# Self-attention of a four-layer Perceiver on one core: scores as row tiles of 32 with masked queries, the bias table added by TensorE, four batches in a group

## The reference, cut to what matters

```python
h = layernorm(x)
q, k, v = heads(h @ Wq), heads(h @ Wk), heads(h @ Wv)      # (16, 16, 64, 16)
s = einsum('bhqd,bhkd->bhqk', q, k) * scale + table[h]     # 64 x 64, -inf above the diagonal
x = x + merge(einsum('bhqk,bhkd->bhqd', softmax(s), v)) @ Wo
```

## Time and profile before

| | us |
|---|---|
| median of 3 runs | 4456.29 |
| lowest, highest | 4456.26, 4457.72 |
| the profiled execution's own time | 4445.81 |
| its span in the trace | 4444.5 |
| mean granted TensorE clock | 0.928 |

### The profile page before, as it was taken

How to read it: one execution, slowest core, us unless ns; L and a number is a source line. 1 busy time by engine, 2 the same in 40 slices (tenths; PEclk the granted TensorE clock), 3 DMA queues, 4 the chain that set the end, 5 groups by cost and what they waited for, 6 DMA issues and landing times. The chain is left out here.

```text
span 4444.5 us, 98901 instructions
## 1 busy us (share of the span) xinstructions
PE 3904.2 (88%) x40956; PEld 3176.0 (71%) x40956; DVE 2984.3 (67%) x7518; ACT 2129.4 (48%) x2970; POOL 1683.7 (38%) x1714
## 2 busy tenths in 40 slices
PE   8999999746999999777899999945797999999766
PEld 6888887425888888447788888823796888888446
DVE  6777777675777777562677777748445777777644
ACT  4555555243555555231455455522463555555334
POOL 3444432201332332320565656413684332322237
PEclk9999999877999999885899999976798999999868
DMA  3212212001111110000211111000552111110025
GB/s 89 61 53 61 53 49 92 16 22 48 31 43 35 39 39 24 22 20 1 78 61 54 46 61 53 24 16 2 186 195 75 37 40 35 43 31 24 16 85 178
DMA packets 126302, 237.48 MB, mean 53 GB/s; under 512 B 10000, under 2 KB 115104, under 8 KB 122016
## 3 DMA queue, kind: packets, MB, share of 16 engines
q1 hardware_dynamic: 118464, 174.11, 13.2%
q0 software_dynamic: 7392, 57.06, 3.7%
HBM read 210.15 MB, written 20.97 MB: 52 GB/s over the span
## 5 line engine op out<-in xcount | busy, mean ns | idle before, releaser
L598 ACT COPY prob_t<-ps 128x1024 f32<-128x1024 f32 x512 | 518.2, 1012 | 1180.1 <-PE ps L485 1180.1
L485 PE MATMUL ps<-c_ident,prob 128*128 128x128 f32 (+1 forms) x6656 | 920.3, 280 | 12.4 <-ACT prob L736 10.6
L485 PEld LDWEIGHTS ps<-c_ident,prob 128*128 128x128 f32 (+1 forms) x6656 | 712.1, 141 | 204.7 <-issue 183.0
L736 ACT ACTIVATE prob<-prob,nmx 128x1601 f32<-128x1601 f32 x512 | 828.6, 1625 | 1.1 <-DVE nmx L649 1.1
L501 PE MATMUL ps<-ctx,wk 128*128 128x400 f32 (+1 forms) x3072 | 688.6, 360 | 25.5 <-DVE vals L608 18.4
L515 PE MATMUL ps<-wv,ctx 128*128 128x256 f32 x4992 | 706.4, 290 | 3.1 <-DVE vals L608 3.1
L515 PEld LDWEIGHTS ps<-wv,ctx 128*128 128x128 f32 x4992 | 619.2, 186 | 16.4 <-DVE vals L608 4.0
L640 DVE CUSTOM_DVE_ANT_0 prob<-ps,mk 128x400 f32<-128x400 f32 (+2 forms) x1024 | 526.2, 570 | 104.0 <-PE ps L473 99.3
L598 DVE COPY prob_t<-ps 128x1024 f32<-128x1024 f32 (+1 forms) x384 | 402.4, 1048 | 270.2 <-PE ps L485 270.2
L643 DVE TENSOR_SCALAR_CACHE_REDUCE prob<-ps 128x400 f32<-128x400 f32 (+2 forms) x1024 | 526.2, 570 | 85.3 <-PE ps L473 79.9
L501 PEld LDWEIGHTS ps<-ctx,wk 128*128 128x128 f32 x3072 | 535.5, 191 | 44.2 <-DVE vals L608 32.9
(11 more groups left out here) (343 smaller groups left out, 4622.8 us busy)
## 6 DMA issues: line engine op xcount, KB each, us to landing
raw_ctx<-in_ctx_t SPq DMA_DIRECT2D x120, 400.0 KB, 3.3
raw_ctx<-in_ctx_t SPq DMA_DIRECT2D x60, 402.0 KB, 5.2
raw_ctx<-in_ctx_t SPq DMA_DIRECT2D x60, 399.0 KB, 3.2
mk<-in_mask_f SPq DMA_DIRECT2D x32, 400.2 KB, 5.4
mk<-in_mask_i SPq DMA_DIRECT2D x16, 800.5 KB, 4.4
sorted<-zeros SPq DMA_DIRECT2D x2, 3840.0 KB, 19.7
rows<-sorted SPq DMA_DIRECT2D x30, 256.0 KB, 5.3
done<-done SPq DMA_DIRECT2D x30, 256.0 KB, 2.5
```

The source lines that it names most:

```text
L485: mm = pe.transpose(ps[0:w, turn_bank(u, i) + a, r * P:(r + 1) * P], prob[u % 2][:, r, x * P:x * P + w], cst['ident'][:])
L598: copy(prob_t[0:w, ring(u, i), 0:nb, :], ps[0:w, turn_bank(u, i):turn_bank(u, i) + nb, :]).then_inc(st[sem], 1)
L736: a.activation(prob[h % 2][:, r, :], prob[h % 2][:, r, :], ACT.Exp, bias=nmx[:, r:r + 1], accum_out=den[h % 2][:, r:r + 1]).then_inc(st['e ...
```

## The change

The core takes groups `G` of four batches, so there are 4 groups in place of 8 pairs.

Scores: in place of masked keys, ACT makes masked queries once for the whole stage: `qm` holds for each pair of neighbouring heads the queries with the other head's 16 rows set to zero. A matmul then contracts 32 rows only, for 2 heads of one batch, and the four groups of 32 rows (`r`) go to four banks of PSUM. The table is added by PE: a matmul of an identity matrix with the table, in the type fp32r, starts each bank, and the scores accumulate on it. For layer 0 the table is in two parts, high and low, so two such matmuls a bank. DVE takes the largest straight from four banks of PSUM (2048 elements a row), subtracts it on the way to SBUF in two halves of 1024, and sums in the same halves. POOL still does the multiplication by the reciprocals.

Values: `vals` holds them in two copies, one for each head of a pair, with zeros in place of the other's; POOL clears it and ACT fills it from PSUM, with SiLU where the layer has it, so that `early_act` and its barrier are gone. Each multiplication by the values takes 16 small matmuls for a transposed part of 4 x 128 columns, where 16 served a whole `u` before.

Output: ACT copies the heads out; the projection of a group (`out`) is done by PE inside the loop, behind the scores of the next group, and DVE adds it to `X` (`add_out`) two groups late, within the loop. The projection uses the PSUM banks of the transposes, so that the first two transposes of group `G` wait for `x_added` of group `G - 1`.

```diff
-    vmask = st.tile("vmask", [P, D])
+    NB = ROWS if L == 0 else 1
+    bias = st.tile("table", [P, NB, 256])
+    bias_parts = [st.tile(f"table{i}", [P, NB, 256], F32R) for i in range(2 if L == 0 else 1)]
...
+    def begin_pool():
+        p = nc.gpsimd
+        p.memset(vals[:], 0.0).then_inc(st['zeroed'], 1)
+        p.tensor_copy(ident_r[:], cst['ident'][:])
+        p.wait_ge(*st.at('weights', 16 * n_loads))
+        p.tensor_copy(bias_parts[0][:], bias[:]).then_inc(st['table_hi'], 1)
...
+        def scores(G):
+            if G:
+                pe.wait_ge(*st.at('shifted', 2 * G))
+            else:
+                pe.wait_ge(*st.at('q_masked', 4 * C))
+            for r in range(ROWS):
+                for i, part in enumerate(bias_parts):
+                    row = part[:, r % part.shape[1], :].unsqueeze(1).broadcast_to([P, 2, 256])
+                    pe.matmul(ps[:, r, :].rearrange("p (a n) -> p a n", a=2), ident_r[:], row, start=(i == 0), stop=False)
+            for a in range(2):
+                for g in range(C):
+                    for bb in range(2):
+                        b, u = 4 * G + 2 * a + bb, UNITS * a + 2 * g + bb
+                        for r in range(ROWS):
+                            rows = slice(32 * r, 32 * r + 32)
+                            mm = pe.matmul(ps[:, r, u * S:(u + 1) * S], qm[rows, g, b].rearrange("p h s -> p (h s)"),
+                                           kt[rows, g, b * S:(b + 1) * S], start=False, stop=(u == 2 * UNITS - 1))
+            mm.then_inc(st['ss_mm'], 1)
...
+            if G and i < 2:
+                pe.wait_ge(*st.at('x_added', 2 * (G - 1) + i + 1))
...
+        scores(0)
+        values()
+        for G in range(GROUPS):
+            if G + 1 < GROUPS:
+                scores(G + 1)
+            if G:
+                out(G - 1)
+            for i in range(4):
+                turn(G, i)
+                if i:
+                    weighted(G, i - 1)
+            weighted(G, 3)
+        out(GROUPS - 1)
...
+        for G in range(GROUPS):
+            largest(G)
+            for a in range(2):
+                shifted(G, a)
+            for a in range(2):
+                totals(G, a)
+            if G >= 2:
+                for u in range(2):
+                    add_out(2 * (G - 2) + u)
+        for t in range(2 * (GROUPS - 2), T):
+            add_out(t)
...
+        exponentials(0)
+        for G in range(GROUPS):
+            if G + 1 < GROUPS:
+                exponentials(G + 1)
+            for i in range(4):
+                a.wait_ge(*st.at('st_mm', 4 * G + i + 1))
+                if 4 * G + i >= 2:
+                    a.wait_ge(*st.at('so_mm', 4 * G + i - 1))
+                a.copy(pt[i % 2][:], ps[:, TURN + i % 2, :]).then_inc(st['pt'], 1)
+            a.wait_ge(*st.at('so_mm', 4 * (G + 1)))
```

More of the change, by code:

```diff
@@ L917, in self_attention @@
     layernorm_act(k, st)
+    begin_pool()
+    st.made(zeroed=1, table_hi=1)
     if row:
@@ L942, in self_attention @@
     OT = st.tile("heads_out", [P, C, NT])
[L943 to L991, removed]
+    qm = st.tile("q_masked", [P, C, B, 2, S])
@@ new lines, in weighted @@
+        def weighted(G, i):
+            a, g = i // 2, i % 2
+            pe.wait_ge(*st.at('pt', 4 * G + i + 1))
+            if i == 0:
+                pe.wait_ge(*(st.at('ot', OUTS * G) if G else st.at('values', 2 * T // 2)))
+            for h in range(2):
+                for bb in range(2):
+                    rows = slice(bb * S, bb * S + S)
+                    for r in range(ROWS):
+                        j = 4 * g + r
+                        mm = pe.matmul(ps[32 * r:32 * r + 32, OUT + bb, i * S:(i + 1) * S],
+                                       vals[rows, 2 * G + a, h, 32 * j:32 * j + 32],
+                                       pt[i % 2][rows, r * P + h * S:r * P + h * S + S], start=(h == 0), stop=(h == 1))
+            mm.then_inc(st['so_mm'], 1)
@@ new lines, in act @@
+        for n in range(T // 2):
+            a.wait_ge(*st.at('sv_mm', n + 1))
+            if n == 0:
+                a.wait_ge(*st.at('zeroed', 1))
+            for h in range(2):
+                o = vals[:, 2 * n:2 * n + 2, h, :].rearrange("p t (j h d) -> p t j h d", h=2, d=HD)[:, :, :, h, :]
+                s = ps[:, TURN + n, :].rearrange("p (t j h d) -> p t j h d", t=2, h=2, d=HD)[:, :, :, h, :]
+                a.activation(o, s, ACT.Silu if L == 2 else ACT.Copy).then_inc(st['values'], 1)
@@ new lines, in exponentials @@
+        def exponentials(G):
+            for x in range(2):
+                p = pr[G % 2][:, :, units(x), :]
+                a.wait_ge(*st.at('shifted', 2 * G + x + 1))
+                a.activation(p, p, ACT.Exp).then_inc(st['sexp'], 1)
+        exponentials(0)
[4 more added lines that the diff above has]
+                a.wait_ge(*st.at('st_mm', 4 * G + i + 1))
+                if 4 * G + i >= 2:
+                    a.wait_ge(*st.at('so_mm', 4 * G + i - 1))
+                a.copy(pt[i % 2][:], ps[:, TURN + i % 2, :]).then_inc(st['pt'], 1)
+            a.wait_ge(*st.at('so_mm', 4 * (G + 1)))
+            for bb in range(2):
+                o = OT[:, :, 256 * G:256 * G + 256].rearrange("p g (x b q) -> p x g b q", x=2, b=2)[:, :, :, bb, :]
+                s = ps[:, OUT + bb, 0:256].rearrange("p (x g q) -> p x g q", x=2, g=C)
+                if bv is None:
+                    a.copy(o, s).then_inc(st['ot'], 1)
+                else:
+                    for g in range(C):
+                        a.activation(o[:, :, g, :], s[:, :, g, :], ACT.Identity, bias=bv[:, g:g + 1]).then_inc(st['ot'], 1)
@@ L1120, in self_attention @@
     pool()
[L1121 to L1129 removed]
+    st.made(q_masked=4 * C, sv_mm=T // 2, values=T, ss_mm=GROUPS, smax=GROUPS, shifted=2 * GROUPS, sexp=2 * GROUPS,
+            total=2 * GROUPS, rtotal=2 * GROUPS, probs=2 * GROUPS, st_mm=4 * GROUPS, pt=4 * GROUPS, so_mm=4 * GROUPS,
+            ot=OUTS * GROUPS, o_mm=T, x_added=T)
     nc.all_engine_barrier()
```

219 lines of the change are left out of this document (86 added, 133 removed).

## The result

The change makes the kernel faster, by 1.2 to 1.3%: median 4396.05 us (4391.08 to 4396.63, four runs) against 4456.27 us (4452.0 to 4457.72, four runs), a ratio of 0.9866 with a 95% interval of 0.985 to 0.9881, 60 us. A second comparison gave 4394.29 for 4447.19 us, 0.9878 (0.9861 to 0.9894), 53 us. The two traces, of executions of 4396.63 and 4445.81 us, lie 49.2 us apart.

What follows compares the result with a forecast made beforehand. DVE's list bounds the cores before, a ring of waiting engines after; cores 40 us less plus 3 around them make 43, median 4456.3 to 4413 us. Forecast 4400 to 4428 (chance 0.55), range 4383 to 4441.

Steps and rivals of the forecast that it cites:

- the high clock: Rival, chance 0.15: PE's clock stays high in the cores; ring 17.1 us, kernel 4382 or so.
- What bounds it: In layer 0's core DVE's list sets the pipeline's round; its work falls from 72 to 38 us a core.
- The ring: In the cores, DVE 8.5, PE 4.7, clock 2.5 and scores 3.9 us follow without overlap: 19.6 us in layer 0.
- the low clock: Rival, sharing chance 0.2 with costlier rings: clock stays low through all of PE's part; about 25 us, 4438.
- Layer 0's core: Start, one full ring and end of layer 0's self-attention core add up to 88.0 us, where before took 87.7.
- my 49.0: Layer 0's core: us into it when DVE's 8.5 us behind group 2's scores end, ahead of one ring of 19.6.
- What closes the ring: PE's transposes of groups 1 and 2 are released by DVE's addition to X, with some 7 us of idling each.
- Layer 2: Layer 2's core goes from 122.0 to 86 us, 36 less, as the separate phase for the values goes.
- The small score matmuls: A group's 32 score matmuls of 32 rows overlap in four row tiles and take 2.2 us, bounds 1.3 and 2.9.
- The rival's 92 us: Rival, chance 0.07: small score matmuls do not overlap, 8.8 us a group, 92 us in four cores, kernel 4505.
- Around the cores: Outside the cores: 3 us less for four stages, bounds 0 and 6; POOL's clearing costs nothing.
- The median: 43 us less takes the profiled 4445.81 to 4403 us and the median 4456.3 to 4413.

Runs made afterwards that it cites:

- the run of layer 2 alone: Layer 2's self-attention as in the kernel after, layers 0, 1 and 3 as before; 4413.92 us, ratio 0.9913 to before.
- copies first: After with DVE's additions to X one turn earlier and ACT's four copies of a group ahead of the next exponentials; 4340.45 us, ratio 0.9752 to before.
- combined: The copies first kernel plus POOL's clearing later and the first group's table matmuls ahead of the wait for masked queries; 4318.95 us, ratio 0.9707 to before.
- the extra matmuls in groups 1 and 2: After with ten unread matmuls behind the output projection, only in the turns of groups 1 and 2; 4387.64 us, ratio 0.9853 to before.

## Why the prediction was right, and where its sizes were off

Against its own trace the sum said 43 us less, and the traces say 49.2. Against the median it said 4413 us, and 4396 was measured: inside the range of 4383 to 4441, but 4 us below the forecast of 4400 to 4428 that had the chance of 0.55. The range was also written a little carelessly: it is said to take in the high clock, which was put at 4382.

- **What bounds it.** Right: DVE's 72 us a core halved, and this did not carry over, because a ring formed.
- **The ring.** 19.6 us predicted in layer 0, 18.05 measured. DVE's part was 7.9 (844.69 to 852.58) for 8.5, the scores 4.05 for 3.9 (840.64 to 844.69; table 2.1 for 1.7, small matmuls 2.01 for 2.2). PE's part with its clock was 5.96 (852.73 to 858.69) for 7.2: I had taken 2.5 us for the clock, and it cost about 1.5, as the same work took 4.5 us in the last group, at full speed. This is the mis-sized term: I had assumed 5 us of work at 1.2 GHz; the clock was 0.50 from about 850.3 to 857.1, the first 2.4 us of that were still idle, and 4.3 us were PE's part, with its copies by ACT between. The clock did fall, so the high clock is out, and it came back within the ring, so the low clock is out.
- **Layer 0's core, 88.0 predicted, 85.6 measured.** Here errors cancelled. The start was dearer than my sum: the first group's scores were done 12.6 us into the core for 10.6 (table 3.78 and scores 3.69, both at a granted clock of 0.50), and the values took 9.4 us for 7.2, at 0.72. By the first addition to `X` of the ring the core was 1.8 us behind my 49.0. The ring gave 1.55 of this back, and the end behind it took 16.8 us for 19.4.
- **What closes the ring.** Half right. The transposes were released by DVE's addition to `X`, as forecast. But it was only the last of two: ACT was done with the next group's exponentials at 850.5 and could have copied from then on, 2 us before the addition's end at 852.6. With the addition out of the way ACT's copy held the ring, at 18.5 us; DVE's list had got longer ahead of the largest, and the exponentials came later with it. My working had ACT's order in layer 0's first group and left it out of the rings.
- **Layer 2.** 36 us predicted for the core, 40.5 there in the traces, 38.7 in the run of layer 2 alone, which also contains the longer stretch ahead of it. The other cores gave 2.1, 4.4 and 4.8 us, 11.3 in all, for 4.
- **The small score matmuls.** Right, with the overlap that the loads of L473 showed. Without it they take 6.69 us. My 8.8, from the transposes' pace, was too dear; the Trainium skill, page "TensorE: Matmul & The Clock Gate", section "LDWEIGHTS (loading the stationary operand)", gives 107 ns for such a load, from which 6.8 us is an estimate for 64 of them: trace and page agree where the clock was 0.91. Where it was 0.50 the 64 took 11.53 us, 180 ns each. The rival's 92 us for the kernel were 105, its mechanism as described, for a smaller price a group at the higher clock (4.7 us more in the third) and a larger one at the lower (7.8 in the first).
- **Around the cores.** Wrong in sign: 3 us less predicted, 4.1 more measured. The step that failed is "POOL's clearing of `vals` ... cost nothing: they lie beside the projections". The clearing lies beside the layer norm, not the projections, and held DVE up there, 2.65 us in each stage. The Trainium skill, page "SBUF — State Buffer", section "Who interferes with whom", has the rule that I left out of the sum: DVE and GpSimd share a pair of ports as a lock for a whole instruction, and DVE's `tensor_scalar` is among the operations that can need it. The trace agrees: 0.17 us became 2.82, up to the end of the 3.51 us of clearing. With it moved, the stretches are 176.8 - 171.1 = 5.7 us shorter than before, inside my bounds of 0 to 6: from the start of the stretch the first projection then comes 0.6, 1.8, 1.0 and 1.4 us earlier than in before, for the 3 us in all that I had taken for the mask's load. Work on an engine that nobody waits for can still cost time, by what its instructions hold up elsewhere.
- **The median.** I added the 10.5 us between before's profiled execution and its median to the forecast. After had no such distance (4396.63 and 4396.05), and before's later medians came down. 10.5 of the 17 us of error are this, the remaining 6 the sizes above. That the range still held 4396 owes something to its width of 58 us, which was meant for the clock and the scores.

## What to carry to other kernels

When the trace names one releaser for a long wait, look for the second one that ends shortly before it: removing the first alone gave nothing here, and changing both orders, with not one instruction more or less, gave as much again as the whole change. Where every engine is only half busy, as here, look at the order first: write each engine's list for one group side by side and ask what stands ahead of the instruction that the others wait for. POOL's clearing was not free, though POOL was idle, because it held up one of DVE's smallest instructions at the head of a stage; and extra work on PE, put there to keep its clock up, paid only where there was a wait.

## What the runs showed of the hardware

- A DVE instruction on 128 by 8 numbers took 2.82 us while POOL cleared 128 by 4096 (3.51 us), and 0.17 us without it. It began 0.72 us into the clearing and ended with it; the `BATCH_NORM_AGGREGATE` instructions just ahead, which ran while the clearing had begun, kept their 0.64 us.
- Matmuls on 32 rows and 64 columns with a load each came at 31 ns a record when they went round four row tiles (granted clock 1.00) and at 105 ns when eight in turn used the same one (0.91); at 0.50 it was 58 and 180 ns.
- In waits of 5.9 to 6.1 us PE's granted clock fell to 0.50 while it still idled, and in after's ring 4.3 us of the time behind the wait ran at it. Behind 1.24 us of idling (copies first, layer 0) and behind 2.95 us (combined, layer 0) it was 1.00. But in the combined kernel's layer 3 it fell behind 1.14 us, and with the extra matmuls in groups 1 and 2 it fell 1 us behind a wait of 1.8 us. So the idling just ahead does not tell by itself whether the clock falls, and what does was not found.
